# A routed block's third chunk of g turned by VectorE in 32x32 squares and carried over DRAM, its products three steps behind, with four output banks

## What is computed

```
x1  = x @ W_base.T + b_base + 2 * sum_e cond[e] * (x @ As[e].T) @ Bs[e].T
top = two largest of softmax(x1 @ gate_w.T), weights normalised to a sum of 2.5
y   = sum over the two experts e: w_e * (silu(x1 @ w_gate[e]) * (x1 @ w_up[e])) @ w_down[e]
out = x + y + (silu(x1 @ sw_gate) * (x1 @ sw_up)) @ sw_down
```

## Time and profile before

| | us |
|---|---|
| median of 3 runs | 497.96 (495.75 to 500.75) |
| span of the profiled execution | 490.9 |
| PE busy | 486.3 |
| PE weight load busy | 450.1 |
| DVE busy | 351.2 |
| ACT busy | 262.0 |
| POOL busy | 220.3 |

### The profile page before, as it was taken

One profiled execution on the slowest core, in us unless ns is written; L12 is line 12 of the kernel. 1 busy time (PEld: TensorE's weight loads), 2 busy tenths in 40 slices (PEclk: granted clock), 3 DMA queues, 4 the chain that ended last, 5 costly groups with the idle time before them and its releaser, 6 DMA issues.

```text
span 490.9 us, 9830 instructions
## 1 busy us (share of the span) xinstructions
PE 486.3 (99%) x3071; PEld 450.1 (92%) x3072; DVE 351.2 (72%) x786; ACT 262.0 (53%) x526; POOL 220.3 (45%) x231
## 2 busy tenths in 40 slices
PE   9999999999999999999999999999999999999997
PEld 8999988888888899999999999999999999888886
DVE  3557866889887547677777767776777776489896
ACT  3577876566563445576555555555554553445322
POOL 2052237655551354655776556556556652211100
PEclk9999999999999999999999999999999999999999
DMA  7498569472222235544444444444444451699932
GB/s 194 152 299 240 174 181 322 152 221 87 44 86 44 87 85 132 127 120 118 125 112 117 128 118 118 118 124 115 114 118 128 120 118 56 174 384 321 385 129 85
DMA packets 104953, 74.53 MB, mean 152 GB/s; under 512 B 61963, under 2 KB 99861, under 8 KB 104917
## 3 DMA queue, kind: packets, MB, share of 16 engines
q1 hardware_dynamic: 97712, 55.20, 38.7%
q0 software_dynamic: 6816, 18.62, 13.1%
q10 hardware_dynamic: 388, 0.27, 0.2%
HBM read 40.25 MB, written 20.32 MB: 123 GB/s over the span
## 4 chain that ended last, share of the span: by engine, by line
PE 99%; DVE 0%; DVEq 0%; issue 0%
PE bank L286 24%; PE bank L287 24%; PE bank L288 24%; PE bank L834 10%; PE bank L836 5%; PE bank L806 5%; PE bank L598 1%; PE bank L610 1%; PE bank L606 1%; PE bank L607 1%; PE bank L629 1%; PE bank L744 1%; PE bank L743 1%; PE bank L762 0%; PE bank L643 0%; PE bank L661 0%
## 5 line engine op out<-in xcount | busy, mean ns | idle before, releaser
L571 POOL DMA_INDIRECT y_rows<-y_sb,dst_i x71 | 70.0, 985 | 74.3 <-DVE y_sb L1411 73.7
L286 PE MATMUL bank<-w_all,rt_h 128*128 x284 | 97.6, 344 | 0.0
L288 PE MATMUL bank<-w_all,rt_l 128*128 x284 | 91.7, 323 | 0.0
L287 PE MATMUL bank<-w_all,rt_h 128*128 x284 | 91.5, 322 | 0.0
L565 POOL DMA_INDIRECT rows<-x_halves,tok_i x71 | 68.6, 967 | 31.1 <-issue 20.9
L834 PE MATMUL bank<-w_all,gt_h 128*128 (+1 forms) x213 | 77.7, 396 | 0.0
L1004 ACT CAST gt_h<-bank 128x512 fp32r<-128x512 f32 (+1 forms) x47 | 27.5, 586 | 85.3 <-DVE bank L1314 76.8
L286 PE MATMUL bank<-xs_h,sg_h 128*128 128x512 f32 x176 | 70.4, 400 | 0.0
L287 PE MATMUL bank<-xs_l,sg_h 128*128 128x512 f32 x176 | 68.9, 391 | 0.0
L288 PE MATMUL bank<-xs_h,sg_l 128*128 128x512 f32 x176 | 68.7, 390 | 0.0
L1398 DVE TENSOR_TENSOR g<-bank,act 128x352 f32<-128x352 f32 x71 | 37.3, 525 | 39.6 <-ACT act L1031 37.7
(11 more groups left out here) (193 smaller groups left out, 1117.9 us busy)
## 6 DMA issues: line engine op xcount, KB each, us to landing
pick<-y_rows SPq DMA_DIRECT2D x16, 512.0 KB, 7.8
x_halves<-x_half SPq DMA_DIRECT2D x8, 512.0 KB, 3.2
xin<-in_x_dram SPq DMA_DIRECT2D x7, 512.0 KB, 5.1
w_own<-in_L_ffn_w_gate_dram SPq DMA_DIRECT2D x8, 352.0 KB, 4.3
w_own<-in_L_ffn_w_up_dram SPq DMA_DIRECT2D x8, 352.0 KB, 4.6
y_sb<-in_x_dram SPq DMA_DIRECT2D x5, 512.0 KB, 3.5
base_rows<-y_sb SPq DMA_DIRECT2D x5, 512.0 KB, 2.8
acc<-base_rows SPq DMA_DIRECT2D x5, 512.0 KB, 7.7
```

Of the source, the lines that this page charges most:

```text
L286: pe.matmul(o, lh, rh, start=start, stop=False, skip_group_check=skip)
L287: pe.matmul(o, lh, rl, start=False, stop=False, skip_group_check=skip)
L288: return pe.matmul(o, ll, rh, start=False, stop=stop, skip_group_check=skip)
L571: pool.indirect_dma_start(y_dram, bass.IndirectOffsetOnAxis(ap=dst_i[:, i:i + 1], axis=0), y_sb[:, i % 4, :], None).then_inc(s_sc[i % 4], 16)
```

## The change

- For the first `NSQ = 67` blocks PE transposes only two chunks of g. `e_high` and `e_low` handle 256 columns instead of 384 for them. The last four blocks (`DIRECT`) go as before.
- The third chunk (96 columns) is turned by VectorE within squares of 32x32, right behind `e_mul` (`squares_of_g`), stored by SP to DRAM (`store_squares`, 128 x 96 elements) and loaded with the squares put at their transposed places (`load_squares`, 96 x 128, in pieces of 32 elements). SP's order becomes `turn_rows(i)`, `load_squares(i-3)`, `store_squares(i-2)`.
- ScalarE makes its high part (`rest_high(i-3)`, between `r_high(i+1)` and `e_silu(i)`), GpSimd its low part (`rest_low`, behind `scatter`).
- PE makes the two products of the third chunk three iterations later: in iteration i after gate and up come `e_down_rest(i-3)`, then the four products of `e_down(i-1)`.
- Since an output bank is open for longer, there are four (`NYE`): banks 4 and 5 join 6 and 7. `e_y` moves from i-2 to i-4 in VectorE's iteration i, the first gathers from five to seven ahead, and GpSimd's wait in the loop from silu of block i+1 to silu of block i+3. The first product into banks 4 and 5 waits for the last shared group before; the shared part behind waits for all `e_y`.

```diff
@@ -54,6 +54,12 @@
     UP = NPRE + NBLK
 
     TURN = 12
+
+    DIRECT = 4
+    NSQ = NBLK - DIRECT
+    MAIN_F = FULL * P
+    LAG = 3
+    NYE = 4
...
+    g_dram = nc.dram_tensor("g_squares", (NSQ, P * REST), F32, kind="Internal").ap()
...
+            sq, gw = [], []
+            for i in range(2):
+                sb(f"pad_sq{i}", [P, MAIN_F], F32, own)
+                sq.append(sb(f"sq{i}", [P, P], F32, own))
+                sb(f"pad_gh{i}", [P, GT - MAIN_F - P], F32, own)
+            for i in range(2):
+                sb(f"pad_gw{i}", [P, FC * P], F32, own)
+                gw.append(sb(f"gw{i}", [P, P], F32, own))
...
-        EG, EU, TB, YE = bank[0], bank[1], bank[2], bank[6:8]
+        EG, EU, TB, YE = bank[0], bank[1], bank[2], [bank[6], bank[7], bank[4], bank[5]]
...
+        done_order = []
+        for n in range(NBLK):
+            if 0 <= n - LAG + 1 < NSQ:
+                done_order.append(n - LAG + 1)
+            if n >= NSQ:
+                done_order.append(n)
+        assert sorted(done_order) == list(range(NBLK))
+
+        def n_done(i):
+            return UE + done_order.index(i) + 1
...
+            def store_squares(b):
+                sp.wait_ge(s_sq, b + 1)
+                sp.dma_start(g_dram[b].rearrange("(p f) -> p f", p=P), sq[b % 2][:, 0:REST]).then_inc(s_sqst, 16)
+
+            def load_squares(b):
+
+                sp.wait_ge(s_sqst, 16 * (b + 1))
+                sp.wait_ge(s_D, n_done(b - 2) if b >= 2 else UE)
+                sp.dma_start(gw[b % 2][0:REST, :].rearrange("p (q r) -> p q r", q=4),
+                             g_dram[b].rearrange("(q p r) -> p q r", q=4, r=32)).then_inc(s_gw[b % 2], 16)
...
             for i in range(4):
                 turn_rows(i)
+            store_squares(0)
             store_base(NPG - 1)
+            load_squares(0)
+            store_squares(1)
             for i in range(4, NBLK):
                 turn_rows(i)
+                if i - 3 < NSQ:
+                    load_squares(i - 3)
+                if i - 2 < NSQ:
+                    store_squares(i - 2)
...
+            def rest_low(b):
+                pool.wait_ge(s_gwh, b + 1)
+                pool.tensor_tensor(gt_l[b % 2][0:REST, REST_COLS], gw[b % 2][0:REST, :],
+                                   gt_h[b % 2][0:REST, REST_COLS].bitcast(F32), ALU.subtract).then_inc(s_gwl, 1)
+
+            for i in range(7):
                 gather(i)
+            for b in range(LAG - 1):
+                rest_low(b)
             for i in range(NBLK):
-                if i + 5 < NBLK:
-
-                    pool.wait_ge(s_act, UE + i + 2)
-                    gather(i + 5)
+                if i + 7 < NBLK:
+
+                    pool.wait_ge(s_act, UE + i + 4)
+                    gather(i + 7)
                 if 14 <= i < 14 + 4 * K:
                     split_low_part(NPG, *divmod(i - 14, 4))
                 scatter(i)
+                if i + LAG - 1 < NSQ:
+                    rest_low(i + LAG - 1)
...
+                if u == UP:
+                    pe.wait_ge(s_y, NBLK)
...
-                for c in range(FC):
+                for c in range(FULL if squared(i) else FC):
...
+            def down_chunk(i, par, to, c, at, e):
+                n = P if c < FULL else REST
+                cols = slice(at, at + P)
+
+                both = w_all[0:n, :, bass.ds(e, 1), GU + c * D:GU + (c + 1) * D].rearrange("p h e d -> p h (e d)")
+                high = w_all[0:n, 0, bass.ds(e, 1), GU + c * D:GU + (c + 1) * D].rearrange("p e d -> p (e d)")
+                pe.matmul(to[:, 0:2 * D].rearrange("p (h d) -> p h d", h=2), gt_h[par][0:n, cols], both,
+                          start=(c == 0), stop=False, skip_group_check=True)
+                return pe.matmul(to[:, 0:D], gt_l[par][0:n, cols], high, start=False, stop=(c == FC - 1),
+                                 skip_group_check=True)
...
+            def e_down(i, at, e):
+
                 pe.wait_ge(s_gl, i + (UE + 1))
-                if not known(i, 2):
-                    pe.wait_ge(s_y, i - 1)
-                for c in range(FC):
-                    n = P if c < FULL else REST
-                    cols = slice(c * P, (c + 1) * P)
-
-                    both = w_all[0:n, :, bass.ds(e, 1), GU + c * D:GU + (c + 1) * D].rearrange("p h e d -> p h (e d)")
-                    high = w_all[0:n, 0, bass.ds(e, 1), GU + c * D:GU + (c + 1) * D].rearrange("p e d -> p (e d)")
-                    pe.matmul(YE[par][:, 0:2 * D].rearrange("p (h d) -> p h d", h=2), gt_h[par][0:n, cols], both,
-                              start=(c == 0), stop=False, skip_group_check=True)
-                    mm = pe.matmul(YE[par][:, 0:D], gt_l[par][0:n, cols], high, start=False, stop=(c == FC - 1),
-                                   skip_group_check=True)
-                mm.then_inc(s_D, 1)
-
-            def e_step(i, par, e_prev, e, following):
+                if known(i, NYE):
+                    if i >= 2:
+                        pe.wait_ge(s_fin, 2 * NPG)
+                else:
+                    pe.wait_ge(s_y, i - (NYE - 1))
+                for c in range(FULL if squared(i) else FC):
+                    mm = down_chunk(i, at % 2, YE[at % NYE], c, c * P, e)
+                if not squared(i):
+                    mm.then_inc(s_D, 1)
+
+            def e_down_rest(i, at, e):
+
+                pe.wait_ge(s_gwl, i + 1)
+                down_chunk(i, at % 2, YE[at % NYE], FC - 1, FC * P, e).then_inc(s_D, 1)
+
+            def e_step(i, at, es, following):
+
                 e_turn_g(i - 1)
-                e_next = e_gate_up(i, par, e, following)
-                e_down(i - 1, 1 - par, e_prev)
-                return e_next
-
-
-            kept = [pe.alloc_register(f"expert{n}") for n in range(2)]
-
-            def keep(*es):
+                e_next = e_gate_up(i, at % 2, es[-1], following)
+                if not known(i, LAG) and squared(i - LAG):
+                    e_down_rest(i - LAG, at - LAG, es[0])
+                e_down(i - 1, at - 1, es[-2])
+                return es[1:] + [e_next]
...
-                sc.copy(gt_h[i % 2][:, 0:FC * P], TB[:, 0:FC * P]).then_inc(s_gh, 1)
+                n = MAIN_F if i < NSQ else FC * P
+                sc.copy(gt_h[i % 2][:, 0:n], TB[:, 0:n]).then_inc(s_gh, 1)
+
+            def rest_high(b):
+
+                sc.wait_ge(s_gw[b % 2], 16 * (b // 2 + 1))
+                sc.copy(gt_h[b % 2][0:REST, REST_COLS], gw[b % 2][0:REST, :]).then_inc(s_gwh, 1)
...
+                if 0 <= i - LAG < NSQ:
+                    rest_high(i - LAG)
...
+            def squares_of_g(i):
+
+                v.wait_ge(s_g, UE + i + 1)
+                if i >= 2:
+                    v.wait_ge(s_sqst, 16 * (i - 1))
+                v.transpose(sq[i % 2][:, 0:REST].rearrange("p (q r) -> p q r", r=32),
+                            g[:, MAIN_F:F].rearrange("p (j q) -> p q j", j=32)).then_inc(s_sq, 1)
+
             def e_y(i):
-                v.wait_ge(s_D, UE + i + 1)
+                v.wait_ge(s_D, n_done(i))
...
+            ys = iter(range(NBLK))
             r_word_low(1)
             e_mul(0)
+            squares_of_g(0)
             r_low(1)
             base(NPG - 1)
             for i in range(1, NBLK):
                 if i + 1 < NBLK:
                     r_word_low(i + 1)
-                if i >= 2:
-                    e_y(i - 2)
+                if i > LAG:
+                    e_y(next(ys))
+                if i == NBLK - 1:
+                    e_y(next(ys))
+                    e_y(next(ys))
                 e_low(i - 1)
                 if i + 1 < NBLK:
                     r_low(i + 1)
                 e_mul(i)
-            e_y(NBLK - 2)
+                if i < NSQ:
+                    squares_of_g(i)
+            e_y(next(ys))
             e_low(NBLK - 1)
-            e_y(NBLK - 1)
+            for b in ys:
+                e_y(b)
...
```

More of the change, by code:

```diff
@@ L117, in adaln_moe @@
             x1_half = [sb(f"x1_half{i}", [P, TG, 2 * D], U16, proj) for i in range(2)]
+        with ExitStack() as own:
+            sq, gw = [], []
[6 more added lines that the diff above has]
+                gw.append(sb(f"gw{i}", [P, P], F32, own))
         gt_h = [sb(f"gt_h{i}", [P, GT], F32R) for i in range(2)]
@@ L238, in adaln_moe @@
         s_y = sem("s_y")
+        s_sq, s_sqst, s_gwh, s_gwl = sem("s_sq"), sem("s_sqst"), sem("s_gwh"), sem("s_gwl")
+        s_gw = [sem(f"s_gw{i}") for i in range(2)]
         s_sc = [sem(f"s_sc{i}") for i in range(4)]
@@ L854, in as_kept @@
                 return [pe.snap(r, min_val=0, max_val=E - 1) for r in kept]
[L856 to L857 removed]
+            first = expert_of(0)
+            es = [first, first, first, e_gate_up(0, 0, first, 1)]
             down(*order[NPRE - 1])
[L859 to L860 removed]
+            HEAD = 5
+            es = e_step(1, 1, es, 2)
+            for n in range(2, HEAD):
+                es = e_step(n, n, es, n + 1)
+            keep(es)
+            n_turns = (NBLK - HEAD - DIRECT) // TURN
```

(7 more changed lines are left out.)

25 lines of the change are left out of this document (9 added, 16 removed).

## The result

| | before | after |
|---|---|---|
| median, us | 497.15 (4 runs) | 559.14 (558.27 to 563.53, 4 runs) |
| ratio, 95% interval | | 1.1247 (1.12 to 1.1295) |
| span of the profiled execution, us | 490.9 | 556.4 |

What follows compares the result with a forecast made beforehand. PE bound the kernel before (99% busy, 3.30 us an iteration); the change would make a GpSimd-ScalarE-DMA loop bind at 4.28. 490.9 span + 62.5 (61.7 loop, -0.7, +1.5) + 7.1 = 560.5, say 560 us; bounds 547 to 581, 8-in-10 range 535 to 590.

Steps and rivals of the forecast that it cites:

- The mechanism: GpSimd's gather waits behind rest_low for ScalarE's copy, which waits for turned rows: a two-iteration loop, 4.28 us each; chance 0.85.
- The sum of 8.55 us: Latency of the loop through ScalarE, GpSimd, gather and turn: 0.91 + 1.14 + 6.5 us for two iterations.
- L1017/L1103 to rest_high's start: ScalarE's queue from joining the turned rows through e_high and r_high to the copy: 0.91 us back to back.
- the pair: Gather's start to ScalarE joining the same block's turned rows, two DMAs in sequence: 6.19 to 6.87, mean 6.5 us.
- my entry and exit terms: Ends of the routed part: first late rows 3.1 us, other half 0.9 closer, 0.7 taken back; net +1.5, before that -0.7.
- the 7.1 us between the span and the median of before: Profiled span 490.9 us lay 7.1 under the median of 497.96; added whole to the forecast.
- What would show it: Signs: PE near 88%, transposes 4.0 to 4.6 us apart, GpSimd and ScalarE waits, PE idle before the third chunk.
- The step on SP: SP's turn plus two new DMA issues take 2.1 us (2.8 at most), under 3.19; its waits only delay the next turn.
- faster, if the pair shortens: Rival: below 4.33 us for the pair, PE stays the limit and 67 x 0.11 are gained: 490.6 us; chance 0.04.
- 1.95 + 0.46 is not the trouble: GpSimd's busy time per iteration plus the new subtraction was no concern; only its place in the queue was.
- a granted clock under 1: Sign that the prediction is wrong; the falling-clock rival put the kernel near 693 us, chance 0.03.
- my estimate of 4.2 for the two: Gather and turn at the skill's fixed 2.0 us per DMA: near 4.2 us, loop 6.3, PE still limiting; rejected for the rows.

Runs made afterwards that it cites:

- e1: Changed kernel with GpSimd's loop order gather(i+7), rest_low(i+1), scatter(i), only rest_low(0) ahead of it; 514.24 us, ratio 1.0342.
- e2: Changed kernel with rest_low moved from GpSimd to VectorE, between r_low and e_mul; 512.80 us, ratio 1.0281.
- e4: Kernel before with one added GpSimd wait, ahead of gather(m) for ScalarE's r_high of block m-2; 544.00 and 537.99 us in its faster runs, ratio 1.0834.
- e10: Changed kernel with two useless 96x128 subtractions on GpSimd between rest_low's wait and its work; 570.08 us, ratio 1.1568.
- e7: Changed kernel without GpSimd's wait for silu ahead of each gather in the loop; 559.47 us, ratio 1.1305.
- e5: e2 with SP's order changed to turn(i), load(i-4), store(i-3); 490.22 us against 493.01 before, ratio 0.9944.
- e9: Changed kernel with only SP's order changed to turn(i), load(i-4), store(i-3); 553.66 us, ratio 1.1229.
- e11: e1 with SP's order of e5; 501.55 us, ratio 1.0162.
- e6: Kernel before with the third transpose of blocks 1 to 66 left out and nothing in its place; 486.78 us against 493.01, ratio 0.9881.
- e3: Changed kernel with one useless 96x128 subtraction on GpSimd behind rest_low's wait, blocks 0 to 63; 553.65 us, ratio 1.1072.

## Why the prediction was right

**The mechanism.** Confirmed by the changed kernel's waits and by three edits: taking the gather out from behind rest_low removes most of the loss (e1, e2), putting only the wait into the kernel before makes most of it (e4). That the loop spans two iterations is borne out by e10, where 0.6 us of extra cost 0.22 an iteration, and by the sum below. Of the chain I had named, e7 shows that the silu wait is not part of it.

**The size of the loop.** The sum of 8.55 us was met exactly, but not by its terms. Means over the blocks of the changed kernel's trace:

```
term                                  forecast   measured
L1017/L1103 to rest_high's start          0.91       1.40
rest_high                                 0.30       0.30
wake-up of GpSimd                         0.08       0.11
rest_low                                  0.46       0.54
to the gather's start                     0.30       0.22
the pair                                  6.5        5.98
sum                                       8.55       8.55
```

The first term missed that ScalarE's queue has PE in it: e_high waits for PE's transposes, and PE itself waits for rest_low (28.7 us in L1113's wait). The pair was too long because both late gathers of the trace of before had the next gather start some 0.5 us ahead of their turns; a turn alone lands in 2.4 us. These are two errors of half a microsecond that cancelled. Two others did in part: the two ends of the routed part cost 3.8 - 0.4 = 3.4 us rather than the 0.8 that my entry and exit terms came to, and of the 7.1 us between the span and the median of before only about 2 lie outside the span (after: 558.27 - 556.4 = 1.9; the kernel before beside e5: 493.01 - 491.1 = 1.9). The other 5 are that the profiled execution of before was faster than the four timed ones. A result within 0.2% is luck; the range was the honest part.

**What would show it.** GpSimd's and ScalarE's waits and PE's idle time before the third chunk were as described. The transposes stood 4.28 us apart on average (within 4.0 to 4.6), but one by one from 3.20 to 7.17, as short and long iterations alternate; the pair was 5.98 against my 6 to 7. PE's share came out at 91%, not 88: PE was "busy" for 508 us instead of 486. Only a part of that is the lowered clock, at which a gate or up product took 374, 347 and 345 ns instead of 344, 322 and 323 (from 220 to 400 us). With two extras these products are back at 348, 326 and 327 ns and PE is still busy for 501.9 us, and with the wait alone, where they are at 343, 322 and 323, for 500.8. So busy time grew with the idle gaps themselves; the durations overlap in an unbroken row of products (0.16 us from start to start), and I take it that what breaks the row adds to what is counted as busy.

**Where it was wrong.** The step on SP. I counted its issue times and found them under 3.19 us, then named the two waits and cost them at nothing, as "the next gather lands later". In the changed kernel SP stands before the load for PE (L398) almost as long in all as before the turn for the gather:

```profile
SPq L389 <- DMA rows<-x_halves,tok_i: 71.4, 55, 3.1
SPq L398 <- PE bank L898: 51.3, 40, 2.0
```

That does no harm there (e9), as it hides behind the larger loop. Without that loop these waits cost 3% (e2 against e5: 1.0281 and 0.9944). So my rival "faster, if the pair shortens" could not have come to its 490.6 us by the pair alone. My "1.95 + 0.46 is not the trouble" for GpSimd left out the gaps around its instructions: its shortest round is 3.21 us, not 2.41, so it too has next to nothing left beside PE's 3.19 (e11).

**The clock.** It did fall, to 0.91 of full on average from 300 to 400 us, between its two levels of 1.2 and 2.4 GHz, while PE idled 14.5 us of the 100, about 0.6 in each 4.3; in the kernel before it was 1.00 there. My prediction had a granted clock under 1 among the signs that the mechanism is wrong. The sign came and the mechanism held, so it was badly chosen. The clock didn't make the loss. The kernel with the wait alone has the same idle share at a clock of 1.00 and an iteration of 4.07 us:

```profile
300.00:400.00 100.00, 85.01 (x515) 76.88 (x513) 56.25 (x123) 39.69 (x100) 47.01 (x49) 1.00 0.35 97
```

and the one with two extras is the slowest of all at a mean clock of 0.988 over its span, where the changed kernel has 0.959. Why one kernel's clock dips and another's doesn't stays open. The Trainium skill ("TensorE: Matmul & The Clock Gate", section "A second HAM failure mode: psum-queue depth-cycling") speaks of such swings; the changed kernel agrees with it, the wait alone from 220 to 400 us does not.

**The price of a DMA.** The Trainium skill ("DMA: Bandwidth & Descriptors", section "Anatomy of one DMA") has about 2.0 us fixed for a DMA that GpSimd issues. My prediction used it for SP's turn as well. The traces have 3.1 us from a gather's start to the turn behind it and 2.4 for a turn with no gather near, more than that for both. By my estimate of 4.2 for the two and my other terms the loop would have hidden behind PE; with the measured pair of 5.98 it could not.

**Small terms.** VectorE's transposition in squares took 0.31 us (0.24 forecast, within its bounds), ScalarE's copy 0.30 (0.30), e_high at 256 columns 0.37 (0.37). The transpose taken from PE is worth 0.09 us a block net (e6), not 0.11.

## What stays open

e5 is at 0.9944 where e6 shows 0.9881 to be possible. Its iteration is 3.25 us against 3.21 in e6. PE idles only 0.5 us from 220 to 400 us in e5, so no long wait of PE makes the difference, and what does is not shown. In e3 the shares of the turns' landing and of the clock were not parted. Nor was it tried to keep gathers and turns apart in time on purpose, which the table of turns suggests.

## What to carry to other kernels

An instruction placed in an in-order queue passes its wait on to everything behind it. Before adding one, find what that next instruction feeds, how many iterations ahead it had been running, and whether the awaited thing itself depends on it: that closes a loop, and the iteration is then the loop's latency divided by the iterations it spans, whatever the engines' shares say. When a mend makes the loop span one iteration more, add up its latency again with every instruction that now lies in it (here the scatter). Count the idle time around each instruction with its duration when asking whether an engine has room, and look for the second wait (here SP's) before claiming what mending the first one gives.

## What the runs showed of the hardware

In the changed kernel the rows of a DMA transpose issued by SP were in use 2.4 us after its start when no indirect gather started within 0.9 us of it, and 3.3 us after it when one did (31 and 30 turns); in e2, with gathers mostly 0.9 to 1.5 us ahead of it, 44 turns took 2.8. This is a good part of why delaying GpSimd by 0.5 us cost no time. The clock granted to PE fell to 0.91 on average in a stretch in which PE idled 14.5% of the time, and stayed at 1.00 in a kernel in which it idled 15%.
